# A graph network on one core: the bound of the indirect DMAs' indices, one register per stage or one load per DMA

## The reference

```python
x = _layernorm(x + _L0_gnn_ref(x, edge_index, edge_weight, W0, b0, W1, b1))   # 2 convolutions of 5 hops each
x = _layernorm(x + _L1_gnn_ref(x, edge_index, ...))   # mean of neighbours, then attention with 4 heads
x = _layernorm(x + _L2_gnn_ref(x, edge_index, ...))   # mean of neighbours
x = _layernorm(x + _L3_gnn_ref(x, edge_index, ...))   # attention with 4 heads
# one hop of the first layer; the others gather rows in the same way
msg = h[row] * norm[:, None]
h = jax.ops.segment_sum(msg, col, num_segments=N_NODES)
```

## Time and profile before

| | |
|---|---|
| time, median of 3 runs | 12,063.8 us (12,035.2 to 12,068.2) |
| span of the profiled execution, first to last instruction | 10,169.1 us |
| what the span leaves out of that median | 1,894.7 us |
| POOL busy | 6,877.8 us (68%) |
| PE busy | 5,803.4 us (57%) |
| DVE busy | 5,533.3 us (54%) |
| ACT busy | 3,168.9 us (31%) |
| indirect DMAs on POOL | 6,651 |
| mean granted TensorE clock | 0.782 of full speed |

### The profile page before, as it was taken

How to read it: one execution, slowest core, us unless ns; L and a number is a source line. 1 busy time by engine, 2 the same in 40 slices (tenths; PEclk the granted TensorE clock), 3 DMA queues, 4 the chain that set the end, 5 groups by cost and what they waited for, 6 DMA issues and landing times. The chain is left out here.

```text
span 10169.1 us, 87608 instructions
## 1 busy us (share of the span) xinstructions
PE 5803.4 (57%) x20243; PEld 3015.6 (30%) x20243; DVE 5533.3 (54%) x16128; ACT 3168.9 (31%) x5401; POOL 6877.8 (68%) x6659
## 2 busy tenths in 40 slices
PE   1573455655555994555555500299786986720387
PEld 0231233323233542222222200144223553410255
DVE  2241455555555655666665668643546884520576
ACT  0352233333332332222222201144343663310144
POOL 7777777777777757777777777774770006767477
PEclk9896677777777996767676755699998997755699
DMA  4620232222224982222222222222333542222353
GB/s 129 202 86 25 75 107 89 91 88 91 88 91 133 262 240 80 89 87 88 85 87 88 85 72 80 70 73 59 70 70 93 166 159 65 74 53 52 88 154 120
DMA packets 1011156, 1016.71 MB, mean 100 GB/s; under 512 B 580468, under 2 KB 634086, under 8 KB 998090
## 3 DMA queue, kind: packets, MB, share of 16 engines
q1 hardware_dynamic: 797770, 880.58, 27.7%
q0 software_dynamic: 212864, 130.53, 7.3%
HBM read 491.67 MB, written 596.27 MB: 107 GB/s over the span
## 5 line engine op out<-in xcount | busy, mean ns | idle before, releaser
L717 POOL DMA_INDIRECT gathered<-u,place_of_source x1564 | 1640.6, 1049 | 524.6 <-issue 476.1
L717 POOL DMA_INDIRECT gathered<-hop,place_of_source x1564 | 1606.0, 1027 | 525.5 <-issue 490.0
L770 DVE SCALAR_TENSOR_TENSOR first_node_sum<-sums,ends_first,first_node_sum 128x64 f32<-128x64 f32 x4290 | 1193.9, 278 | 8.4 <-DVE sums L760 7.2
L746 DVE TENSOR_TENSOR weighted<-gathered,bank 128x512 f32<-128x512 f32 (+1 forms) x490 | 335.3, 684 | 1466.7 <-DMA gathered<-hop,place_of_source 639.8
L760 DVE SCALAR_TENSOR_TENSOR sums<-sums,same_as_before,weighted 128x64 f32<-128x64 f32 x3510 | 972.0, 277 | 62.0 <-DVE weighted L746 39.3
L717 POOL DMA_INDIRECT gathered<-x,row_of_source x782 | 804.9, 1029 | 293.8 <-issue 225.5
L2228 POOL DMA_INDIRECT out_dram<-lane_out,node_to_write x392 | 407.9, 1041 | 251.9 <-ACT lane_out L2149 139.4
L487 PE MATMUL bank<-dense_tmp,mean 128*128 128x512 f32 x980 | 523.7, 648 | 58.8 <-ACT dense_tmp L496 55.1
L717 POOL DMA_INDIRECT pair<-h_sage,row_of_source x391 | 403.3, 1032 | 224.3 <-issue 124.0
L487 PE MATMUL bank<-dense_a,center 128*128 128x512 f32 x588 | 441.0, 842 | 192.7 <-DVE dense_a L511 153.8
L717 POOL DMA_INDIRECT gathered<-y,place_of_source x391 | 406.3, 1039 | 189.6 <-issue 118.8
(11 more groups left out here) (460 smaller groups left out, 15228.9 us busy)
## 6 DMA issues: line engine op xcount, KB each, us to landing
head_sums<-head_sums SPq DMA_DIRECT2D x98, 1024.0 KB, 4.8
y<-conv_out SPq DMA_DIRECT2D x294, 256.0 KB
conv_out<-y SPq DMA_DIRECT2D x245, 256.0 KB, 3.1
hop<-sums SPq DMA_DIRECT2D x196, 256.0 KB, 2.1
turned<-rows_turned SPq DMA_DIRECT2D x196, 256.0 KB, 2.7
cat<-turned SPq DMA_DIRECT2D x196, 256.0 KB
u<-conv_out SPq DMA_DIRECT2D x196, 256.0 KB, 2.0
lane_raw<-x SPq DMA_DIRECT2D x196, 256.0 KB
```

What stands on the lines that cost most here:

```text
L717: return e.indirect_dma_start(out=into, out_offset=None, in_=tab, in_offset=bass.IndirectOffsetOnAxis(ap=index, axis=0), bounds_check=top, ...
L746: e.tensor_tensor(weighted[g % 2][:, 0:n, :], st.rows_of(g), over(st.weight[:, cols], D), ALU.mult).then_inc(st.weighed.handle, 1)
L770: e.scalar_tensor_tensor(h, row_, flast[:, t:t + 1], h, ALU.mult, ALU.add).then_inc(st.headed.handle, 1)
```

## The change

The bound is loaded with `to_reg` once ahead of each loop, and the register is handed to each DMA. The two gathers of `first_sum` keep their number. Nothing else is changed.

```diff
     def stage_gpsimd(e, st):
+        top = e.to_reg(st.top)
         for g in range(NG):
...
-                gather(e, st.table, st.index[:, t:t + 1], into, st.top).then_inc(st.gathered[g % RING].handle, 16)
+                gather(e, st.table, st.index[:, t:t + 1], into, top).then_inc(st.gathered[g % RING].handle, 16)
...
             def xc_gpsimd(e):
                 e.wait_ge(*dst_in(48))
+                last_row = e.to_reg(N - 1)
...
-                        gather(e, x, dsti[:, t:t + 1], flat(ring[i])[:, k * D:(k + 1) * D], N - 1).then_inc(xc_got[i].handle, 16)
+                        gather(e, x, dsti[:, t:t + 1], flat(ring[i])[:, k * D:(k + 1) * D], last_row).then_inc(xc_got[i].handle, 16)
...
             def place_gpsimd(e):
...
+                last_place = e.to_reg(N * XW // 2 - 1)
                 for t in range(T):
...
-                                         in_=own[:, t, :], in_offset=None, bounds_check=N * XW // 2 - 1,
+                                         in_=own[:, t, :], in_offset=None, bounds_check=last_place,
...
                     e.wait_ge(*last_moved(1))
+                    last_row = e.to_reg(CB + RP - 1)
...
-                            gather(e, hh, comb[:, t:t + 1], pair[i % RING][:, k, D:PW], CB + RP - 1).then_inc(got[i % RING].handle, 16)
+                            gather(e, hh, comb[:, t:t + 1], pair[i % RING][:, k, D:PW], last_row).then_inc(got[i % RING].handle, 16)
...
                 def _(e):
+                    last_row = e.to_reg(CB + RP - 1)
...
-                            gather(e, x3, comb[:, t:t + 1], rows_[g % RING][:, k, :], CB + RP - 1).then_inc(got[g % RING].handle, 16)
+                            gather(e, x3, comb[:, t:t + 1], rows_[g % RING][:, k, :], last_row).then_inc(got[g % RING].handle, 16)
...
                 def _(e):
+                    last_node = e.to_reg(N - 1)
...
-                                in_=W.out[0][0][:, k * D:(k + 1) * D], in_offset=None, bounds_check=N - 1,
+                                in_=W.out[0][0][:, k * D:(k + 1) * D], in_offset=None, bounds_check=last_node,
```

## The result

The changed kernel takes 11,902.0 us (median of 4 runs, 11,856.6 to 11,959.0), the kernel before beside it 12,066.0 (4 runs, 12,035.2 to 12,092.1): a ratio of 0.986, interval 0.983 to 0.989. Forecast were 12,060 us and no difference.

What follows compares the result with a forecast made beforehand. POOL's rate of issuing indirect DMAs was taken as the bound. Stage starts -(0 to 11), L1041 -(0 to 4), rest 0: likeliest -4 us on the span; with 1,894.7 us carried over, 12,060 us, range 11,990 to 12,110.

Steps and rivals of the forecast that it cites:

- The median carried over: Whole run: the 1,894.7 us by which the timed median exceeds the profiled span were kept unchanged in the forecast.
- Where the wait ends late: Output stage, 44 POOL waits for ACT: gaps may shrink from 0.95 to about 0.45 us, gaining nothing since PE sets the rate.
- Removed: POOL's sequencer: 6,631 MOVEs of 29 ns go, taken as 0 ns each in steady state; at most 181 us.
- The counter-example of rows 8: POOL from 2738.1 to 2740.4 us: no MOVE, yet two gaps total 0.6 us, so MOVEs were judged off the path.
- The waits: Heads of DMA groups: waits move from MOVE to DMA or an own instruction; taken as 0, at most 423 us slower.
- Stage starts: About 14 places where POOL starts after a wait: taken as 0, at most 11 us saved.
- long gaps of L1041: Scatter: three gaps of 2.95 us instead of 0.30 may come half as often, saving 0 to 4 us.
- The faster rival: Each MOVE's 29 ns lies on POOL's path: 181 us saved, 11,883 us; chance 0.10 in whole or in part.

Runs made afterwards that it cites:

- h2: Changed kernel with the last wait ahead of each group written twice, slow condition: 12,112.2 us, ratio 0.9915 to the kernel before.
- h1: The changed kernel itself, measured again in the slow condition: 12,046.8 us, ratio 0.9853 to the kernel before.
- e3: Changed kernel with the last wait ahead of each group written twice, on an earlier occasion: 11,944.8 us, ratio 0.9882 to the kernel before.
- h3: Changed kernel with 5,816 already met waits added between POOL's DMAs, slow condition: 12,159.6 us, ratio 0.9950 to the kernel before.
- e2: Changed kernel with a MOVE, carrying the wait, back ahead of each group's first DMA only: 11,966.3 us, ratio 0.9904 to the kernel before.

## Why the prediction was wrong

- *The median carried over.* This is the step that failed: "The median of the runs, 12,063.8, is 1,894.7 us longer than the span. The trace doesn't say what lies there; I carry it over unchanged". The time lies inside the span of the runs that were timed, as 1,569 us of late waits of POOL that the trace did not have. The trace was of a run of about 10,171 us, the times were of runs under other conditions, and the sum was made for the first. Carried over as a constant, those 1.9 ms were taken to be out of the change's reach; the time shrank by 164 us. For the condition of the trace the sum holds: no difference to speak of was forecast, and the two kernels measured 10,173.4 and 10,172.1 us.
- *Where the wait ends late.* The mechanism was named and right: "such a gap can shrink from 0.95 to about 0.45 us"; it shrank to about 0.45 (0.77 from release to DMA became 0.27). "It gains nothing" was sized by 44 waits of the output stage, all that the trace had. The timed runs have about 180 more, for DVE, in stages whose rate POOL sets. Worth up to 65 us of 172 (h2 against h1; their intervals don't meet), and by the rows at most 88 for the start itself; the pauses that come through in h2 and not in h1, some 21 us, are in the same 65.
- *Removed: 0 ns for a MOVE.* Right in the quick condition, with 11 and 12 runs at 1.000, and the regular gap is 0.30 us in both. In the slow condition it was wrong: taking the MOVEs out from between the DMAs while the wait stays late gained 0.85% (h2) to 1.18% (e3). "What hides it is the queue ahead of the engine", the prediction said, and "Were the cover gone, the MOVE would cost its 29 ns". A MOVE does not always take 29 ns: in `source_row` of the slow kernel before the median is 0.70 us, and the gaps there are 25 us longer in all than after the change. The counter-example of rows 8 was sound as far as it went; it was a pause of the sequencer that the queue covered, and it did not say what happens where the cover is gone. Most of what the MOVEs cost in the slow condition stays unexplained.
- *The waits: 0, bound 423 us.* The sign was the other way: a DMA that carries a wait starts 0.50 us sooner, not later. It is 0.26 us from release to start, against 0.755 when a MOVE of the sequencer waits. And the gaps of the quick traces stay at 0.305 us with 5,816 instructions more, each with a wait that is met.
- *Stage starts, long gaps of L1041: 0 to 15 us.* Nothing to be told from zero; the three gaps of 3.0 us in the scatter are still three, with half the instructions, 113 DMAs apart in every profile.
- *The rivals.* The faster rival (MOVE on the path, 11,883 us) is near the result by its number and not by its mechanism: it asked for gaps of 0.27 us everywhere, and the regular ones stayed 0.30. That 181 us and the measured 164 are close is luck.

What stays open: why h3 costs 113 us, when the gaps that theory L can claim make up some 20; why e2 and e3 gain 1% with the late start of before; why some MOVEs take 0.70 us; and what makes the slow condition. For the first, kernels were there, but met only the quick condition; the others were not tried.

## What to carry to other kernels

If the profiled execution's span and the timed runs differ by far more than the runs among themselves, here by 1,895 us against 33, the profile may be of another condition: ask what each wait that is just met in it would cost if it were late, and don't carry the difference over as a constant. In this kernel the sequencer's work was hidden where its waits ended early (ratios 0.9997 to 1.0004). Where they ended late it paid to put the wait on the DMA itself (h2 took 65 us more than h1) and to keep other instructions of that engine from between the DMAs (h3 took 113 us more). The edit cost nothing where nothing was late, and gained 1.4% where things were. A look at the same DMA number in several kernels tells a pause that belongs to the place from one that an edit made.

## What was not expected of the hardware

- The same program has two times, 10,162 to 10,175 us and 12,066 to 12,218 us as medians of 21 to 35 and of 4 to 20 runs, and one chip showed both. Three single runs in the quick condition (11,817 and 12,457 us with met waits added, 19,515 us for the changed kernel) are in no ratio. In the slow condition the granted clock over the span is 0.73 to 0.74 against 0.78, but PE's busy time makes up only 76 of the 493 us by which the hops are longer; DVE goes on late with PE's results (idle time ahead of L479: 884.2 us against 27.3), and the stretch in which POOL issues no indirect DMA takes the same 730 us in both (729.8 and 729.7). That the DMAs or the recording are the cause was not tried.
- An indirect DMA that carries its wait itself started 0.26 us after the release, against 0.755 when a MOVE carried the wait and 0.741 when a wait instruction stood there (medians at the gathers).
- The sequencer pauses by the number of DMAs, not of instructions: about every 80th gather two MOVEs are 2.5 us apart, in the quick traces of the kernel before with and without 5,816 met waits. At the second DMA of a gather's group it shows as a gap behind a late wait, 1.43 to 1.57 us as the median of each slow trace, the changed kernel's apart, with or without an instruction between the DMAs. The scatter has three gaps of 3.0 us, 113 DMAs apart, with or without MOVEs.
- A MOVE of POOL takes 29 ns in the quick traces, but 0.70 us as the median of the 390 in `source_row` in the slow trace of the kernel before.
